# Layer 0's back mix in three fp32r products, with the token values projected later and three tiles turned ahead

## The reference

```
char2sub = softmax(Q_char K_sub^T * scale) V_sub            # tokens over the context: "forward"
sub2char = softmax(Q_sub K_char^T * scale) V_char           # context over tokens: "back"
sub2char = interp_linear(sub2char, 512)                     # two context rows for each token, mixed
gate     = sigmoid([char2sub, sub2char] Wg^T + bg)
x        = x + tanh(g) * (gate * char2sub + (1 - gate) * sub2char)
```

## Time and profile before

| | |
|---|---|
| time, median of 3 runs | 1373.46 us (1373.07 to 1375.33) |
| the profiled execution | 1375.52 us, span 1373.7 us |
| mean granted TensorE clock | 0.985 |
| busy PE | 1316.8 us (96%) |
| busy DVE, ACT, POOL | 779.8 (57%), 735.2 (54%), 482.7 us (35%) |

### The profile page before, as it was taken

One profiled execution on the slowest core, in us unless ns is written; L12 is line 12 of the kernel. 1 busy time (PEld: TensorE's weight loads), 2 busy tenths in 40 slices (PEclk: granted clock), 3 DMA queues, 4 the chain that ended last, 5 costly groups with the idle time before them and its releaser, 6 DMA issues. The chain is left out here.

```text
span 1373.7 us, 25412 instructions
## 1 busy us (share of the span) xinstructions
PE 1316.8 (96%) x9798; PEld 1235.8 (90%) x9798; DVE 779.8 (57%) x1738; ACT 735.2 (54%) x1405; POOL 482.7 (35%) x378
## 2 busy tenths in 40 slices
PE   5999999999989999999999998999999999999996
PEld 5987969879669999999999998999999889999996
DVE  6566786785773535445445234576776865356322
ACT  5365465555545556555555554455554645666644
POOL 0101001000026646556556543120210256677533
PEclk9999999999989999999999999999999999999998
DMA  7102031220335536445353334031212276564322
GB/s 248 41 12 93 21 126 47 68 93 1 101 105 137 151 54 154 117 89 147 73 139 64 53 61 125 0 126 51 83 36 93 78 228 167 111 167 110 55 46 41
DMA packets 73676, 127.49 MB, mean 93 GB/s; under 512 B 7952, under 2 KB 53664, under 8 KB 73504
## 3 DMA queue, kind: packets, MB, share of 16 engines
q1 hardware_dynamic: 46816, 81.92, 18.1%
q0 software_dynamic: 26688, 43.34, 16.8%
HBM read 100.44 MB, written 24.79 MB: 91 GB/s over the span
## 5 line engine op out<-in xcount | busy, mean ns | idle before, releaser
L2622 DVE TENSOR_TENSOR m_hidden_lo<-m_act_out,m_hidden_hi 128x512 fp32r<-128x512 f32 x224 | 154.8, 692 | 351.8 <-ACT m_hidden_hi L2551 308.3
L434 PE MATMUL banks<-m_down_hi,m_hidden_hi 128*128 128x256 f32 x896 | 259.0, 289 | 1.2 <-DVE m_hidden_lo L2622 0.8
L434 PE MATMUL banks<-m_down_lo,m_hidden_hi 128*128 128x256 f32 x896 | 255.2, 285 | 0.0
L434 PE MATMUL banks<-m_down_hi,m_hidden_lo 128*128 128x256 f32 x896 | 255.2, 285 | 0.0
L434 PE MATMUL banks<-m_xt_hi,m_up_hi 128*128 128x256 f32 x640 | 184.1, 288 | 2.1 <-issue 2.1
L434 PE MATMUL banks<-m_xt_hi,m_up_lo 128*128 128x256 f32 x640 | 180.7, 282 | 0.0
L434 PE MATMUL banks<-m_xt_lo,m_up_hi 128*128 128x256 f32 x640 | 180.6, 282 | 0.0
L434 PEld LDWEIGHTS banks<-m_down_hi,m_hidden_hi 128*128 128x128 f32 x896 | 171.7, 192 | 5.8 <-DVE m_hidden_lo L2622 1.5
L434 PEld LDWEIGHTS banks<-m_down_lo,m_hidden_hi 128*128 128x128 f32 x896 | 171.6, 192 | 0.0
L434 PEld LDWEIGHTS banks<-m_down_hi,m_hidden_lo 128*128 128x128 f32 x896 | 171.5, 191 | 0.0
L2707 POOL DMA_INDIRECT m_other_block<-rows,list_i x84 | 94.8, 1129 | 153.8 <-DVE list_i L1606 88.4
(11 more groups left out here) (390 smaller groups left out, 3421.7 us busy)
## 6 DMA issues: line engine op xcount, KB each, us to landing
stage<-in_up SPq DMA_DIRECT2D x22, 512.0 KB
stage<-in_down SPq DMA_DIRECT2D x21, 512.0 KB
stage<-in_ctx_rows SPq DMA_DIRECT2D x20, 512.0 KB
stage<-in_ctx_cols SPq DMA_DIRECT2D x24, 402.0 KB
m_stage<-in_down SPq DMA_DIRECT2D x10, 512.0 KB
m_stage<-in_up SPq DMA_DIRECT2D x9, 512.0 KB
rows<-xn SPq DMA_DIRECT2D x8, 528.0 KB, 3.3
stage<-in_ctx_picked SPq DMA_DIRECT2D x8, 512.0 KB
```

The lines of the kernel that those rows point to most:

```text
L434: mm = q.e.matmul(dst, a, b, start=first and n == 0, stop=last and n == 2, skip_group_check=True)
L2622: q.e.tensor_tensor(lo, m.act[(n * HP + h) % ACTS], f32(hi), ALU.subtract).then_inc(*hidden_lo.mark((layer, n, h)))
```

## The change

The back mix is made of high and low parts and of three fp32r products. For this the token values and the turned probabilities get low parts, made by DVE (`vector_back_values`, `vector_turn_pc`), and new places in SBUF (`back_operands`), over memory that is not in use at that time. PE now waits for low parts in `tensor_back_mix`, and the PSUM banks of both are free when the low parts are made. The projection of the values moves from step 2 behind the back scores of step 5 on PE and ACT. Three tiles are turned ahead instead of two. On ACT tile 2 is copied before pieces 1 to 3. On DVE the four low parts stand ahead of pieces 1 and 2.

```diff
+        def back_operands(m):
+
+            with ExitStack() as st:
+                sb("back_hold0", [P, 3 * KD * TOK], F32, st)
+                m.vb = sb("back_values", [P, TT, D], F32R, st)
+                sb("back_hold1", [P, 7 * KD * TOK], F32, st)
+                m.pct_hi, m.vb_low = [], []
+                for i in range(2):
+                    m.pct_hi.append(sb(f"back_probs_t{i}", [P, 2, TOK], F32R, st))
+                    m.vb_low.append(sb(f"back_values_low{i}", [P, 2, D], F32R, st))
+                    sb(f"back_pad{i}", [P, CTXP - 3 * TOK], F32, st)
+            m.pct = [(m.pct_hi[j % 2][:, j // 2, :], m.s3[1 - j % 2][:, j // 2, :]) for j in range(TT)]
...
 def tensor_back_values(q, b):
-                bank, emptied = gen.take(use, his, use)
+                bank, emptied = gen.take(use, los, use)
...
+        def vector_back_values(q, b, h):
+            use = ("vb", 0, b, h)
+            q.wait_ge(*turned_probs.of(0, b, TT - 1, 2))
+            dve_low(q, use, a0.vb_low[h][:, :, :].rearrange("p t d -> p (t d)"), gen.of(use), high_values(h))
...
 def tensor_turn_pc(q, b, j):
-            bank, emptied = gen.take(use, his, use)
+            bank, emptied = gen.take(use, los, use)
...
+        def vector_turn_pc(q, b, j):
+            use = ("pc", b, j)
+            dve_low(q, use, a0.pct[j][1], gen.of(use), a0.pct[j][0])
...
         def tensor_back_mix(q, b, j):
-            q.wait_ge(*his.of("pc", b, j))
-            q.wait_ge(*his.of("vb", 0, b, 1))
+            q.wait_ge(*los.of("pc", b, j))
+            q.wait_ge(*los.of("vb", 0, b, 1))
             if j == 0:
                 q.wait_ge(*back_exped.of(b, 1, KD - 1))
             for m in range(KD):
-                mm = q.e.matmul(ps[:, m, :], a0.vb[:, j, m * P:(m + 1) * P], a0.pct[j], start=j == 0, stop=j == TT - 1,
-                                skip_group_check=True)
+                mm = three(q, ps[:, m, :], (a0.vb[:, j, m * P:(m + 1) * P], a0.vb_low[j // 2][:, j % 2, m * P:(m + 1) * P]), a0.pct[j],
+                           j == 0, j == TT - 1)
...
 tensor_attention_0
                     elif i == 2:
-                        tensor_back_values(q, b)
...
                         tensor_back_scores(q, b, 0, 3)
+                        tensor_back_values(q, b)
...
                 tensor_turn_pc(q, b, 0)
                 tensor_turn_pc(q, b, 1)
+                tensor_turn_pc(q, b, 2)
                 for j in range(TT):
                     tensor_back_mix(q, b, j)
-                    if j + 2 < TT:
-                        tensor_turn_pc(q, b, j + 2)
+                    if j + 3 < TT:
+                        tensor_turn_pc(q, b, j + 3)
...
 scalar_attention_0
                     elif i == 5:
                         scalar_back_scores(q, b, 0, 2)
                         scalar_back_scores(q, b, 0, 3)
+                        scalar_back_values(q, b, 0)
+                        scalar_back_values(q, b, 1)
...
                 convert(q, "a", pieces[0:1])
                 scalar_turn_pc(q, b, 0)
                 scalar_turn_pc(q, b, 1)
+                scalar_turn_pc(q, b, 2)
                 convert(q, "a", pieces[1:3])
...
                 convert(q, "a", pieces[3:4])
-                scalar_turn_pc(q, b, 2)
                 scalar_turn_pc(q, b, 3)
...
 vector_attention_0
                         vector_back_scores(q, b, 0, 3)
+                        vector_back_values(q, b, 0)
+                        vector_back_values(q, b, 1)
                         picks_free(q, b, 1)
                         convert(q, "d", [("pick", b, 1)])
...
                 convert(q, "d", pieces[0:1])
+                vector_turn_pc(q, b, 0)
+                vector_turn_pc(q, b, 1)
                 if b and more:
                     vector_mark(q, 0, b - 1, 0)
-                    vector_mark(q, 0, b - 1, 1)
                 elif b:
                     vector_put(q, 0, b - 1, 0)
+                vector_turn_pc(q, b, 2)
+                if b and more:
+                    vector_mark(q, 0, b - 1, 1)
+                vector_turn_pc(q, b, 3)
                 convert(q, "d", pieces[1:3])
                 if b:
                     vector_mark(q, 0, b - 1, 2)
                     vector_mark(q, 0, b - 1, 3)
```

More of the change, by code:

```diff
@@ L314, in attention_memory @@
                 m.gate_w = sb(n + "gate_weights", [P, 2 * KD, D], F32, st)
-                m.vb = sb(n + "token_values", [P, TT, D], F32, st)
+                m.staged = sb(n + "token_values", [P, TT, D], F32, st)
                 m.cv = sb(n + "mixed_values", [P, KD, TOK], F32, st)
@@ L331, in attention_memory @@
                 m.diff = m.probs[1][:, 0:KD * TOK].rearrange("p (k t) -> p k t", k=KD)
-                m.pct = [m.probs[j % 2][:, j // 2 * TOK:(j // 2 + 1) * TOK] for j in range(TT)]
                 m.x = [sb(n + f"x{i}", [P, TT, D], F32, st) for i in range(2)]
@@ L398, in build @@
         att[0].stack.close()
+        back_operands(att[0])
         ops[0].stack.close()
@@ L444, in build @@
         slots_0 = Ring(list(enumerate([*own_stage, xn.rearrange("p t d -> p (t d)")[:, 0:STAGE],
-                                       *(v.rearrange("p a c -> p (a c)") for v in (att[0].cv[:, :, :], att[0].vb[:, :, :]))])))
+                                       *(v.rearrange("p a c -> p (a c)") for v in (att[0].cv[:, :, :], att[0].staged[:, :, :]))])))
         slots_1 = Ring(list(enumerate([*own_stage, *att[1].stage])))
@@ L1184, in scalar_back_values, with high_values @@
             q.wait_ge(*projected.of(*use))
-            act_high(q, use, a0.vb[:, 2 * h:2 * h + 2, :].rearrange("p t d -> p (t d)"), gen.of(use))
+            act_high(q, use, high_values(h), gen.of(use))
+        def high_values(h):
+            return a0.vb[:, 2 * h:2 * h + 2, :].rearrange("p t d -> p (t d)")
+        def vector_back_values(q, b, h):
+            use = ("vb", 0, b, h)
+            q.wait_ge(*turned_probs.of(0, b, TT - 1, 2))
+            dve_low(q, use, a0.vb_low[h][:, :, :].rearrange("p t d -> p (t d)"), gen.of(use), high_values(h))
         def tensor_back_scores(q, b, which, i):
@@ L1268, in scalar_turn_pc @@
             q.wait_ge(*turned_pc.of(b, j))
-            act_high(q, use, a0.pct[j], gen.of(use))
+            act_high(q, use, a0.pct[j][0], gen.of(use))
+        def vector_turn_pc(q, b, j):
+            use = ("pc", b, j)
+            dve_low(q, use, a0.pct[j][1], gen.of(use), a0.pct[j][0])
         def tensor_back_mix(q, b, j):
-            q.wait_ge(*his.of("pc", b, j))
-            q.wait_ge(*his.of("vb", 0, b, 1))
+            q.wait_ge(*los.of("pc", b, j))
+            q.wait_ge(*los.of("vb", 0, b, 1))
             if j == 0:
@@ L1887, in scalar_attention_0 @@
                         scalar_turn_mix(q, 0, b, i - 2)
-                    if i == 2:
-                        scalar_back_values(q, b, 0)
                     if i < TT:
@@ L1902, in scalar_attention_0 @@
                     elif i == 2:
-                        scalar_back_values(q, b, 1)
                         if b:
```

## The result

The changed kernel took 1398.88 us (median of 4 runs, 1395.32 to 1402.72). Beside it the kernel before took 1374.39 (4 runs, 1373.07 to 1375.47). The ratio is 1.0177, 95% interval 1.0156 to 1.0197: slower by 24.5 us, where I had forecast 17, with a range to 1396. The profiled execution of after took 1402.72 us (span 1400.9), the longest of its four.

A forecast was written before the change was run, and what follows sets the result against it. The prediction took PE to bound layer 0's attention, with a ring of context loads as second chain. Gate delays 12.1, values +1.1 and clock +4.0 made about +17 on 1373.5: 1390.5, say 1390 us; range 1380 to 1396.

The forecast's parts named there:

- batch 0, gate late: Second half of batch 0's gate starts later behind the late mix evacuation, arithmetic gain already taken off: +3.3 us.
- batches 1 and 2, gate late: The same delay of the gate's second half, at 202.85 instead of 200.12 in batch 1: +2.7 us each.
- batch 3, gate late without the clock: Lists' addition and marks queue behind low parts on DVE, delaying the gate +3.1; with the gather's +0.3, +3.4 us.
- values moved, net: Values' projection behind the first back scores: bank waits cost 2.0, covered waits save 0.9; net +1.1 us.
- clock: PE's granted clock falls behind new idle stretches: 1.2 us in each of batches 0 to 2, 0.4 in batch 3.
- all else, in the median: Everything behind layer 0's attention was taken to carry its difference over in full, with no added time.
- The ring: Three context slots in layer 0: late low part delays p4's load, ScalarE's mix evacuation and the gate; +3.3 in batch 0.
- The arithmetic: In the back mix, 96 fp32r matmuls replace 32 float32 ones: 5.1 us less PE work, 1.3 a batch.
- the 0.3 for it: Batch 3: first expert block's gather may land after PE wants to turn it; +0.3 us, bounds 0 and 2.
- the two waits that I had as covered: PE's waits for the second picked columns, 0.9 us in total, would be covered by the moved values' projection.
- Doubled falls: Rival: two clock stretches per batch, or last batch's delay uncovers routing at layer 0's end; 1396 to 1402, chance 0.06.

The follow-up runs named there:

- Experiment 1: Changed kernel with VectorE making piece p1's low part ahead of the fourth turned tile's low part; 1386.64 us, ratio 1.0104 to the kernel before.
- experiment 2: Changed kernel with ScalarE evacuating the back mix before it converts piece p4; 1388.49 us, ratio 1.0125 to the kernel before.
- experiment 6: Changed kernel with only the high parts' product issued in the back mix, 64 of 96 matmuls left out, low parts still made; 1400.75 us, ratio 1.0172.
- experiment 4: Changed kernel with batch 3's lists' addition and last two marks ahead of the turned tiles' low parts on VectorE; 1398.12 us, ratio 1.0189.
- values_moved: Kernel before with only the token values' projection moved behind the first back scores, no low parts; 1375.02 us, ratio 0.9986.
- experiment 7: Same run as values_moved: kernel before with only the token values' projection moved; 1375.02 us, ratio 0.9986.
- mix_out_first: Same run as experiment 2: changed kernel with ScalarE evacuating the back mix before converting piece p4; 1388.49 us, ratio 1.0125.
- Experiment 3: Changed kernel with small matmuls that nobody reads put into PE's idle time in batches 0 to 2; 1385.54 us, ratio 1.0104.
- filled: Same run as Experiment 3: changed kernel with unread small matmuls in PE's waits of batches 0 to 2; 1385.54 us, ratio 1.0104.
- p1_ahead: Same run as Experiment 1: changed kernel with piece p1's low part made ahead of the fourth turned tile's; 1386.64 us, ratio 1.0104.
- tile3_ahead: Changed kernel with ScalarE copying the fourth turned tile before it converts piece p3; 1401.67 us, ratio 1.0181 to the kernel before.

## Why the prediction was right in direction and short in size

The direction and the mechanism held. By terms, against layer 0's attention, where all of them lie:

| term | forecast | measured |
|---|---|---|
| batch 0, gate late | +3.3 | +2.9 |
| batches 1 and 2, gate late | +2.7 each | +2.5 each |
| batch 3, gate late without the clock | +3.4 | +3.0 |
| values moved, net | +1.1 | +0.5 |
| clock | +4.0 | +8.7 |
| sum | +17.2 | +20.1 |
| all else, in the median | 0 | some +4, open |

*The ring.* Each step came at its place, within 0.6 us: the fourth low part ends at 107.73 (forecast 108.1), the load is issued at 108.66 (109.05), ACT has p4 at 112.07 (112.6), and the gate starts at 113.75 (114.3). The errors are all of one sign, since p3 landed 0.35 sooner than in the kernel before. Experiment 1 shows the cause by removing it, experiment 2 by making its lateness harmless.

*The arithmetic.* The mix ends at 109.5, as forecast, 1.4 sooner after its first turn than in the kernel before. The gain exists (experiment 2: 8.35 against 9.47), and is lost in after because PE isn't what ends last there (experiment 6).

*Batch 3.* The third turn waits 1.77 us for the lists and the puts 1.71 and 0.78 for the marks, as forecast. The gather of the first expert block was covered, so the 0.3 for it was not needed; that cover goes when the gate comes earlier (experiment 4).

*The values.* The forward values wait 0.54, 0.53 and 0.53 in batches 0 to 2, where I had 0.5 (by the distance of starts in batch 0, against values_moved, it is 0.7). In batch 3 they don't wait, but the back scores for the upper picks do, 0.52, one of the two waits that I had as covered. Against that the move won back more than the 0.9 that I had counted: 1.8 by experiment 7. The net was +0.5.

*The clock: the term that was mis-sized.* I took 1.2 us for each of batches 0 to 2 and 0.4 for batch 3, and set 1.7 a batch as the upper bound, from a single fall. The falls in batches 0 and 2 stayed through the whole gate. They cost 2.56 and 2.90, above the bound; batch 1's cost 1.61. In batch 3 the fall met the mix: ten records from 391.61 on stand 0.31 to 0.43 apart instead of 0.231, in sum some 1.6 (mix_out_first, with the same waits and no fall, is 1.5 shorter there). The wrong step was to take one observed fall for the longest: the grant in the earlier trace rows is low inside two stretches of 3 us, that of batch 0 from 112 to 119 us. A longer fall already stood in the trace of the kernel before, behind a stretch in which PE mostly waits (windows view):

```profile
405.00:408.00 3.00, 1.04 (x25) 0.81 (x25) 2.48 (x5) 0.53 (x1) 0.00 (x0) 0.80 0.94 321
408.00:411.00 3.00, 3.00 (x14) 3.00 (x15) 2.97 (x6) 0.00 (x0) 1.82 (x2) 0.50 0.09 20
411.00:414.00 3.00, 3.00 (x17) 3.00 (x17) 1.24 (x2) 0.00 (x0) 2.39 (x3) 0.56 0.37 101
```

Summed as for the earlier trace rows it is (0.20 + 0.50 + 0.44) x 3 = 3.4 us, and 2.8 of them from 408 on, where PE is at work: more than the 1.7 that I had set as the bound.

Doubled falls were in the text as a rival, at 0.06, and that rival's time is the one that came, in part by luck: the falls of batches 0 and 2 were twice as long as that of the earlier trace rows, but that alone gives 1394.5 (below). Experiment 3 shows that the clock's share is this large: with PE kept busy, 7.0 us go away while the waits stay.
The Trainium skill (TensorE: Matmul & The Clock Gate, Terms) puts the penalty at the throttled time times what the clock loses. The rows agree only for the part in which PE has work: in batch 0, PE was still waiting when the grant fell at 112, and that part cost nothing, so 2.56 us were lost of the 3.4 that half of the throttled time would be.

*The rest: the term that was put at nothing.* With the terms of the attention alone, the result would have been 1374.4 + 20.1 = 1394.5, inside the range. The other 4 us put it outside. "Everything behind layer 0 waits for it, so the difference carries over in full" took the time outside the attention as unchanged. The medians show it 4.4 us longer in after, and 3.5 to 9.7 longer in the edited kernels except filled; what makes it longer stays open. I had no term for spread in stages that the change doesn't touch either, although the profile that I summed against was one execution.

## What to carry to other kernels

A cheaper matmul form helps only where PE ends last; here its low parts went into DVE's queue in front of the conversions that free a load's buffer, and the load's lateness came back through ACT. When an in-order engine gets new work, list what stands behind it, and put whatever releases a buffer or a bank ahead of whatever waits for a distant producer: moving one conversion took back 14 of the 20 us. Where PE got some 4 us of new waiting here, in one piece or broken by small puts, the work behind it lost another 1.6 to 3 us at half rate; small matmuls in the wait bought that back. So add such a term, and look through the whole trace for its longest fall before setting its bound.

## What the runs showed of the hardware

The grant fell in front of gates for which PE had waited 4.08 us (batch 0; granted clock 0.50 and 0.51 from 113 to 119 us), and also in batch 1, where small puts broke the wait (gate stretch 4.73). It held at 1.00 in p1_ahead, whose wait was 1.2 us, and in filled, where 25 small matmuls filled the same wait. The half-rate time after a similar wait isn't fixed: batch 1 took 4.73 us for its gate in after and 6.11 in tile3_ahead, and batch 0 5.70 and 4.70. Nor does the same wait always bring a fall: batch 3 has the same waits of PE in after, where the grant fell at 392 us, and in mix_out_first, where it didn't. A float32r matmul of 512 columns went from 0.231 us apart to 0.43 at half rate. The load of 512 KB took 3.4 us from issue to use (108.66 to 112.07), and 3.6 before the change (105.10 to 108.69).
